# Windowed attention on one core: projections a tile further ahead, k spread first in GpSimd's turn, first rows loaded first, variances inverted by a power

## The reference

```python
x = x + attn(layernorm(x))            # layernorm: (x - m) / sqrt(var + 1e-5)
# attn: 16 heads of 8 channels, qkv = xn @ Wqkv.T + bqkv
scores = einsum('bhid,bhjd->bhij', q, k) / sqrt(8)
mask = (j <= i) & (j >= i - 31)       # 32 keys seen by each query
probs = softmax(where(mask, scores, -inf))
y = einsum('bhij,bhjd->bhid', probs, v) @ Wo.T + bo
```

## Time and profile before

| | |
|---|---|
| time, median of 3 runs | 2317.53 us (2315.78 to 2321.61) |
| the profiled execution: its own time | 2313.75 us |
| its span, first to last instruction | 2312.0 us |
| busy over the span | PE 90%, DVE 66%, POOL 61%, ACT 52% |
| attention stage | 0 to about 272 us |

### The profile page before, as it was taken

The page is one execution under the profiler, slowest core; times in us unless marked ns, Lnnn a source line. Parts: engine busy times, 40 slices in busy tenths (PEclk is TensorE's granted clock), DMA queues, the critical chain, the costliest instruction groups (busy, mean ns, idle before and its releaser), DMA issues. The chain is left out here.

```text
span 2312.0 us, 45713 instructions
## 1 busy us (share of the span) xinstructions
PE 2091.6 (90%) x16030; PEld 1594.5 (69%) x16031; DVE 1515.2 (66%) x2651; ACT 1212.7 (52%) x2405; POOL 1416.4 (61%) x891
## 2 busy tenths in 40 slices
PE   5787799999999988998998988998869999999998
PEld 4666544799999934665665666665644469999994
DVE  5666567333333376999999999999965733333335
ACT  4555422222222228999998898889822222222222
POOL 3555300366766614999998999989840026767660
PEclk9999999999999998899999899999879999999999
DMA  7000000000000132322332223232224000000014
GB/s 283 2 0 0 16 22 3 12 25 25 24 25 24 23 99 96 106 94 93 93 100 94 87 94 101 95 97 93 93 79 184 3 10 26 24 25 24 25 24 113
DMA packets 72184, 141.96 MB, mean 61 GB/s; under 512 B 9947, under 2 KB 43741, under 8 KB 69766
## 3 DMA queue, kind: packets, MB, share of 16 engines
q1 hardware_dynamic: 62982, 121.87, 15.8%
q0 software_dynamic: 9088, 18.63, 2.9%
HBM read 123.82 MB, written 16.65 MB: 61 GB/s over the span
## 5 line engine op out<-in xcount | busy, mean ns | idle before, releaser
L1815 POOL TENSOR_TENSOR m_seen<-m_state,experts 128x1024 f32<-128x1024 f32 x256 | 599.5, 2361 | 70.9 <-DVE m_state L1867 67.8
L1867 DVE TENSOR_TENSOR_SCAN m_state<-experts,m_ps 128x512 f32<-128x512 f32 x448 | 540.4, 1233 | 3.5 <-PE m_ps L1446 2.0
L1042 PE MATMUL f_up_ps<-f_xT,f_weights 128*128 128x128 f32 x3976 | 489.0, 277 | 10.1 <-issue 7.1
L1042 PEld LDWEIGHTS f_up_ps<-f_xT,f_weights 128*128 128x128 f32 x3976 | 469.8, 193 | 16.2 <-issue 16.0
L1165 POOL DMA_INDIRECT f_xin<-tokens,f_take x142 | 141.1, 994 | 363.1 <-DVE f_take L812 252.2
L1463 PE MATMUL m_ps<-ident,m_seen 128*128 128x128 f32 x2048 | 301.7, 296 | 30.9 <-POOL m_seen L1815 30.9
L1463 PEld LDWEIGHTS m_ps<-ident,m_seen 128*128 128x128 f32 x2048 | 264.4, 154 | 74.2 <-POOL m_seen L1815 47.4
L851 DVE TENSOR_TENSOR f_hT<-f_gated,f_up_ps 128x512 f32<-128x512 f32 x142 | 97.6, 687 | 326.9 <-ACT f_gated L941 326.9
L941 ACT ACTIVATE f_gated<-f_up_ps 128x512 f32<-128x512 f32 x142 | 84.9, 598 | 410.1 <-PE f_up_ps L1042 410.1
L1646 ACT ACTIVATE experts<-m_delta,experts 128x512 f32<-128x512 f32 x448 | 291.9, 714 | 1.0 <-DVE m_delta L1893 0.5
L1082 PE MATMUL f_y_ps<-experts,f_hT 128*128 x2272 | 277.1, 275 | 0.9 <-DVE f_yout L864 0.9
(11 more groups left out here) (257 smaller groups left out, 3231.8 us busy)
## 6 DMA issues: line engine op xcount, KB each, us to landing
experts<-m_rows SPq DMA_DIRECT2D x144, 512.0 KB, 3.7
experts<-in_experts SPq DMA_DIRECT2D x17, 1461.0 KB, 18.1
tokens<-f_rows SPq DMA_DIRECT2D x8, 512.0 KB, 4.9
f_rows<-expert_out SPq DMA_DIRECT2D x8, 512.0 KB, 7.4
f_cols<-expert_out SPq DMA_DIRECT2D x8, 512.0 KB, 7.3
f_xin<-tokens,f_take POOLq DMA_INDIRECT x142, 2.6
expert_out<-f_yout,f_back_to POOLq DMA_INDIRECT x142, 2.2
X<-in_x SPq DMA_DIRECT2D x4, 512.0 KB, 5.9
```

The source lines that it names most:

```text
L1042: mm = pe.matmul(up_ps[:, bank + k, col:col + P], weights[:, s, at:at + P], xT[:, s, :], start=True, stop=True)
L1815: pool.tensor_tensor(seen[:, n % SEEN], state[:, n % RING], c_rep[:, Q % C_RING, n % C_GROUP, :].unsqueeze(1).to_broadcast([P, HALF, SEG]) ...
L1867: dve.tensor_tensor_scan(state[:, n % RING, h, :], decay_, drive_, before_, ALU.mult, ALU.add).then_inc(s_state, 1)
```

## The change

- TensorE's and ScalarE's projection work (transposed xn, q, k, v) is done for tile t+3 in the turn of t, layernorm (xn) for t+4; `run` begins at -4.
- GpSimd's turn begins with k_spread of t+2, ahead of the subtraction and the totals.
- SyncE loads the first tile of each batch first (one DMA of 256 KB), then five small loads, then the other 28 tiles (four DMAs), then woT, bo and ones with a semaphore of their own. The bias product comes after tile 0's projection, its copy after tile 0's v.
- Square root and reciprocal of the variances go. GpSimd takes var to the power -0.5 as a guess, VectorE improves it with one Newton step and makes `shift` (four dependent operations). This is done three times: for round 0, for round 1, and for the rest. The rest's row statistics are taken in VectorE's turns 0 to 2 (8 tiles in each), behind L451, and its inverses in turn 3.

```diff
         def load_first_x(sp):
+            sp.dma_start(x_s[:, :, 0, :], x_d[:, :, 0, :]).then_inc(first_x_in, 16)
         def load_x(sp):
+            for b in range(B):
+                sp.dma_start(x_s[:, b, 1:TPB, :], x_d[:, b, 1:TPB, :]).then_inc(x_in, 16)
...
+                small = [(bqkv[:], "bqkv"), (ident[:], "ident"), (wqkvT[:], "wqkvT"), (own_head[:], "own_head"),
+                         (mask[:].rearrange("p f k -> p (f k)"), "mask")]
+                outer = [(woT[:], "woT"), (bo[:], "bo"), (ones[:], "ones_row")]
...
-                    for r in range(-3, B):
+                    for r in range(-4, B):
...
                     def _(pool):
                         pool.memset(one[:], 1.0)
+                        pool.memset(power[:], -0.5).then_inc(s_zero, 1)
                         pool.memset(v[:], 0.0).then_inc(s_zero, 1)
+                        def guesses(nth, of):
+                            pool.wait_ge(s_var, nth)
+                            pool.tensor_tensor(of(guess[:]), of(rstd[:]), of(power[:]), ALU.pow).then_inc(s_guess, 1)
+                        guesses(1, first_round)
                         pool.wait_ge(small_in, SMALL)
-                        pool.wait_ge(s_bias, 2)
                         def body(n, r):
+                            if alive(n, r + 2):
+                                t = at(n, r + 2)
+                                pool.wait_ge(s_qk, t + 1)
+                                wait(pool, s_score, t - 1)
+                                pool.tensor_tensor(k_spread[:, s], ...).then_inc(s_spread, 1)
+                                if isinstance(t, int) and t == 0:
+                                    guesses(2, second_round)
...
+                                if isinstance(t, int) and t == B - 1:
+                                    guesses(3, later_rounds)
...
                     def _(act):
-                        deviations(act, s_var, s_std, 1, first_round)
...
-                            if alive(n, r + 2):
+                            if alive(n, r + 3):
                                 act.wait_ge(s_x_turned, t + 1)
...
+                            if alive(n, r + 4):
+                                t = at(n, r + 4)
+                                act.activation(xn[:, r % 2, :], ...).then_inc(s_ln, 1)
+                                if isinstance(t, int) and t == B - 1:
+                                    act.wait_ge(s_shift, 2)
+                                if isinstance(t, int) and t == 2 * B - 1:
+                                    act.wait_ge(s_shift, 3)
...
                     def _(dve):
-                        dve.wait_ge(x_in, 64)
+                        dve.wait_ge(first_x_in, 16)
...
+                        def shifts(nth, of):
+                            r0, g, var = of(guess[:]), of(apart[:]), of(rstd[:])
+                            dve.wait_ge(s_guess, nth)
+                            dve.tensor_tensor(g, r0, r0, ALU.mult).then_inc(s_newton, 1)
+                            dve.wait_ge(s_newton, 3 * nth - 2)
+                            dve.scalar_tensor_tensor(g, g, -0.5, var, ALU.mult, ALU.mult).then_inc(s_newton, 1)
+                            dve.wait_ge(s_newton, 3 * nth - 1)
+                            dve.scalar_tensor_tensor(var, g, 1.5, r0, ALU.add, ALU.mult).then_inc(s_newton, 1)
+                            dve.wait_ge(s_newton, 3 * nth)
+                            dve.scalar_tensor_tensor(of(shift[:]), of(mean[:]), -1.0, var, ALU.mult, ALU.mult).then_inc(s_shift, 1)
+                        sums(range(1))
+                        variances(dve, s_stats, s_var, first_round)
                         shifts(1, first_round)
+                        dve.wait_ge(x_in, 64)
+                        sums(range(1, 2))
+                        variances(dve, s_stats, s_var, second_round, 2)
+                        shifts(2, second_round)
...
+                                if isinstance(t, int) and t < 2:
+                                    sums(range(2 + 2 * t, 4 + 2 * t))
+                                if isinstance(t, int) and t == 2:
+                                    sums(range(6, 8))
+                                    variances(dve, s_stats, s_var, later_rounds, 3, summed[0] + 1)
+                                if isinstance(t, int) and t == B - 1:
+                                    shifts(3, later_rounds)
...
                     def _(pe):
-                            if alive(n, r + 2):
+                            if alive(n, r + 3):
                                 pe.wait_ge(s_ln, t + 1)
                                 wait(pe, s_v, t)
...
+                                v_of(r + 3).then_inc(s_qkv, 1)
+                                if isinstance(t, int) and t == 0:
+                                    pe.wait_ge(outer_in, OUTER)
+                                    pe.matmul(turn_ps[:, 0, :], bqkv[:, 2:3].to_broadcast([P, P]), woT[:], start=True, stop=False)
+                                    pe.matmul(turn_ps[:, 0, :], ones[:], bo[:], start=False, stop=True).then_inc(s_bias, 1)
```

More of the change, by code:

```diff
@@ L233, in attention @@
                 s_yT, s_wo, s_x = ts("yT"), ts("wo"), ts("x")
[L235 to L238, removed]
+                small = [(bqkv[:], "bqkv"), (ident[:], "ident"), (wqkvT[:], "wqkvT"), (own_head[:], "own_head"),
+                         (mask[:].rearrange("p f k -> p (f k)"), "mask")]
+                outer = [(woT[:], "woT"), (bo[:], "bo"), (ones[:], "ones_row")]
+                ZEROED = 3
+                SMALL, OUTER = 16 * len(small), 16 * len(outer)
                 def at(n, r):
@@ L371, in body @@
                                 ins.then_inc(s_v, 1)
[L372 to L378, removed]
+                                if isinstance(t, int) and t == 0:
+                                    act.wait_ge(s_bias, 1)
+                                    act.activation(bias[:], turn_ps[:, 0, :], ACT.Copy).then_inc(s_bias, 1)
+                            if alive(n, r + 4):
+                                t = at(n, r + 4)
+                                j = tile(n, r + 4)[0]
+                                act.activation(xn[:, r % 2, :], X[:, ds(j * D, D)], ACT.Identity, bias=shift[:, ds(j, 1)], scale=rstd[:, ds(j, 1)]).then_inc(s_ln, 1)
+                                if isinstance(t, int) and t == B - 1:
                                     act.wait_ge(s_shift, 2)
+                                if isinstance(t, int) and t == 2 * B - 1:
+                                    act.wait_ge(s_shift, 3)
                         run(act.Fori, body)
@@ L385, in _, with sums @@
                         dve.memset(kT[:], 0.0).then_inc(s_zero, 1)
-                        dve.wait_ge(x_in, 64)
[L387 to L398, removed]
+                        dve.wait_ge(first_x_in, 16)
+                        def sums(rounds):
+                            for k in rounds:
                                 for b in range(B):
                                     row_sums(dve, k + b * TPB)
+                                summed[0] += B
+                        def shifts(nth, of):
[10 more added lines that the diff above has]
+                        variances(dve, s_stats, s_var, first_round)
                         shifts(1, first_round)
+                        dve.wait_ge(x_in, 64)
+                        sums(range(1, 2))
+                        variances(dve, s_stats, s_var, second_round, 2)
+                        shifts(2, second_round)
                         dve.wait_ge(small_in, SMALL)
@@ L458, in _ @@
                         pe.wait_ge(small_in, SMALL)
-                        pe.matmul(turn_ps[:, 0, :], bqkv[:, 2:3].to_broadcast([P, P]), woT[:], start=True, stop=False)
-                        pe.matmul(turn_ps[:, 0, :], ones[:], bo[:], start=False, stop=True).then_inc(s_bias, 1)
                         spread_count, mask_count, turned_count = (pe.alloc_register(x) for x in ("spread_count", "mask_count", "turned_count"))
```

79 lines of the change are left out of this document (36 added, 43 removed).

## The result

The changed kernel takes 2279.93 us (median of 4 runs, 2275.33 to 2285.45) against 2318.81 us (4 runs) before: ratio 0.9834, 95% interval 0.9808 to 0.9859. The profiled execution is the slowest of the four, 2285.45 us, span 2283.7.

A forecast was written before the change was run, and what follows sets the result against it. It took a chain across engines, scores to k_spread, to bound the attention turn. 29.8 us from 25 shorter turns plus 7 from the start made 36.8 less, so 2280 us as a median; range 2267 to 2298.

The forecast's parts named there:

- The circle: Attention loop: chain from scores through GpSimd's k_spread to the next scores sets the turn, 7.56 us; the change cuts it.
- The new turn: Attention loop after the change: TensorE's own work sets a turn of 6.4 us, bounds 6.1 and 6.9; 29.8 us less.
- two registers: Register sets ahead of L495 in the loop, until now in idle time: 0.2 us a turn, up to 0.4.
- the jump: Loop jump after four turns: 0.24 us stays visible, at most 1.5 us per four turns; 0.1 taken per turn.
- The other circles: Attention loop: chains over exp (5.7 us) and over totals (5.6 us) stay below the new turn.
- The start: Before the loop: first rows early and no square root bring score 6 7 us earlier, bounds 3 and 11.
- The third power: Turn 3, ahead of exp of tile 4: power 0.5 us, four VectorE operations 0.9; score 6 near 61 us.
- The bound of 6 us: Upper bound on GpSimd's power in the start, forecast at 0.5 us on 4 columns; lower bound 0.2.
- the prediction's own signs of being wrong: L495 or L513 wait over 0.3 us each turn; power above 2 us; turn 6.9 with gaps; granted clock under 1.00.
- The rule on first calls: GpSimd's power in the start: a freshly loaded routine's first call pays about 6 us; if so, 2286.7 us.
- The slow-power rival: Start: the power takes several us, once or each time; at 6 us once, 2287 us; chance 0.10.
- the rival on the other side: Attention stage: TensorE's clock falls to 1.2 GHz, kernel slower than before, 2332 us at 14 turns; chance 0.04.

The follow-up runs named there:

- experiment 1: Changed kernel with k_spread moved back behind subtraction and totals in GpSimd's turn, projections still a tile ahead: 2319.23 us, ratio 0.9995 to the kernel before.
- experiment 2: Kernel before with only k_spread moved to the top of GpSimd's turn, nothing projected ahead: 2308.09 us, ratio 0.9952 to the kernel before.
- experiment 7: Transpose of the totals done twice each turn: in the changed kernel 2284.59 us, ratio 0.9845; in the kernel before 2319.35 us, ratio 1.0001.
- experiment 5: Changed kernel again, 2276.20 us, beside variants: third power early 2275.96; square root instead 2276.74; early power with later bias product 2274.39; that with ScalarE's shift wait moved 2272.80.
- Experiment 4: Changed kernel with the third power replaced by a product of the same operands (later rounds wrongly normalised): 2277.04 us, ratio 0.9808 to the kernel before.
- experiment 6: Changed kernel with k_spread of tile 6 held until the third shift is done: 2280.24 us, ratio 0.9841 to the kernel before.
- the variant where TensorE had stood 1.68 and 0.27 us there: Changed kernel with early third power, bias product a turn later, and ScalarE's third-shift wait moved ahead of xn of tile 8: 2272.80 us, ratio 0.9808.

## Why the prediction was right, and where it was not

The time, 2280 against 2279.93, and the total of the stage, 36.8 against 36.7 us, came out. Two of its terms did not; they erred against each other by about 5.6 us, so the closeness of the total is partly luck.

- **The circle** scores, mask, maximum, subtraction, totals, k_spread was the bound, and it needs both edits to be cut. Shown by experiments 1, 2 and 7. It also showed that the wait at L495 named "issue" was k_spread's.
- **The new turn.** Forecast 6.4 us (6.11 + 0.2 for two registers + 0.1 for the jump), measured 6.18 twice and 6.26 twice in each pass of the loop, 6.22 in the mean. The terms that were too large are the registers and the jump. From the output product to the next scores it takes 0.42 us in the loop (104.27 to 104.69), where two registers are set between them, and the same behind the loop, in a turn that sets none:

```profile
216.16 0.49 PE L573 MATMUL y_ps<-woT,yT 128*128 128x128 f32 x2
216.58 0.71 PE L524 MATMUL score_ps<-k_spread,qT 32*32 32x256 f32 x32
```

  That turn takes 6.18 us too, so the registers ahead of the scores cost nothing that can be seen, and neither does the jump: the turn that ends with it is one of those of 6.18. The 0.08 us of the other two lie inside the product with v (L498 to L573 takes 2.13 instead of 2.05); why is open. With the last turn, which the forecast counted like the others, that makes 35.4 us instead of 29.8.
- **The other circles** (exp 5.7, totals 5.6) stayed below, as worked out: no wait of TensorE for either in the loop.
- **The start.** xn of tile 0 forecast at 8.3, measured 7.63: right, with its parts off: the rows landed at 3.7, not 5, and the power took 1.06, not 0.5. The 3.7 us that the forecast read as the root's cost were 2.0: for the other 1.7 ScalarE stood behind the bias product and its copy (13.35, in the rows of experiment 5), which the change moved out of the way as well. Score 0 forecast at 17.4, measured 18.69 (woT, bo and ones landed at 13.4, not 11.6). exp of tile 0 forecast at 24 to 25.4, measured 25.52.
- **The third power.** "Power 0.5, four operations 0.9": measured 4.18 and 2.1. This is the step that failed, and tile 6 came 1.3 us earlier instead of 7. The bound of 6 us was in the text, but as the price of one first call; that a power costs per column was mentioned and then not used for the 24. In the profile 4 columns take 1.02 to 1.06 and 24 take 4.18: (4.18 - 1.02) / 20 = 0.16 us a column, an estimate from two sizes. Experiment 4 shows that 4 us of the loss are the power; experiments 5 and 6 that 1 us is VectorE's operations beside GpSimd; the rest is TensorE's lower clock after the stop: from L544 to the next scores it takes 6.53 us (60.84 to 67.37) where 5.2 were forecast. Two of the prediction's own signs of being wrong came true here, a power row above 2 us and a granted clock under 1.00.
- **The rule on first calls.** The first power takes 1.06 us and the second 1.02. The Trainium skill (GPSIMD Engine Reference, Instruction dispatch) has about 6 us for the first call of a freshly loaded routine; here the measurement decides: none is seen. The slow-power rival happened, in another form than told: the time goes with the columns, not with the first call. Its 2287 us did not come, because the loop was faster than forecast.
- **The clock.** In the loop it is 1.00 at 97% busy, so the rival on the other side did not come. It fell where the prediction did not look, in the stop ahead of turn 4.

Still open: what decides in which turn of the start the clock comes up (2 us), and why the up-projection took 5.3 us more in some executions than in others, beyond that the clock is lower there (0.93 granted in the 127.7 us behind the attention of the changed kernel, 235.6 to 363.3, and 0.97 in the 127.7 us behind that of the kernel before, 272.3 to 400.0).

## What to carry to other kernels

Write down the circle through the engines link by link before moving work ahead: an operation leaves it only when both its input is early enough (projected a turn ahead) and its place in its engine's order is (first), and either alone may give nothing. Then work out the next longest circle, or the sum of one engine's stream, because that is the new turn. And price a one-time step with the size it has there: six times the columns was four times the power, on the way of everything behind it.

## What the runs showed of the hardware

- GpSimd's power (tensor_tensor) costs 1.02 to 1.06 us for 128x4 and 4.18 us for 128x24, a product of 128x24 0.24 us.
- A VectorE operation with two operands in on-chip memory beside a GpSimd operation ended only as that one ended: 24 columns took 1.47 us beside the subtraction and 1.18 beside k_spread, and 0.18 alone (L425 of experiment 6). The Trainium skill (GPSIMD Engine Reference, Key points) names contention with VectorE operations of two such inputs; these rows agree. Operations with one operand in PSUM did not lengthen: the mask addition takes 1.22 beside k_spread, as before the change without it.
- TensorE's granted clock was 1.00 in 24 turns at 97% busy. It was at 0.50 (1.2 GHz) after the stop of 7.1 us ahead of L544 in turn 4, and even in the variant where TensorE had stood 1.68 and 0.27 us there (0.51 granted from 54 to 56 us). Yet the 1.3 us at which it stood in every turn of the kernel before left it at 1.00; what sets the two apart no run shows. Where the clock fell, the stop cost its own length and the slower products behind it.
- In the first 35 us the granted clock of the changed kernel's profile reads 1.00 throughout, while L544 takes 1.12 us at 26.62 and 0.60 in the loop: there the length of a known product tells more of the clock than that reading.
